# Attention slots of an audio tower: bulk transfers moved out of slots 66 to 100, second-half q and k products moved later

## The reference

```
h = tok(x)                      # rows t, t+3, t+6 side by side (768) times W, plus b: 8 x 744 x 256
h = h + attn(layernorm(h))      # q, k, v products, 16 heads of 16, causal softmax, times Wp, plus bp
h = h + ffn(layernorm(h))       # 4 experts, the best 2 per token by router logits, gelu between w1 and w2
```

## Time and profile before

| | |
|---|---|
| median of 3 runs | 1852.43 us |
| profiled execution | 1851.91 us, its span 1850.2 us |
| TensorE busy | 1545.8 us, 84% |
| VectorE, ScalarE, GpSimd busy | 1098.0, 710.4, 834.7 us |
| granted TensorE clock, mean | 0.904 of full speed |
| DMA | 256.23 MB, mean 138 GB/s |

### The profile page before, as it was taken

How to read it: one execution, slowest core, us unless ns; L and a number is a source line. 1 busy time by engine, 2 the same in 40 slices (tenths; PEclk the granted TensorE clock), 3 DMA queues, 4 the chain that set the end, 5 groups by cost and what they waited for, 6 DMA issues and landing times.

```text
span 1850.2 us, 33109 instructions
## 1 busy us (share of the span) xinstructions
PE 1545.8 (84%) x10648; PEld 1197.0 (65%) x10648; DVE 1098.0 (59%) x3458; ACT 710.4 (38%) x1463; POOL 834.7 (45%) x912
## 2 busy tenths in 40 slices
PE   2679798788798798797797895469999999999997
PEld 2536464464474375464463441469999999999997
DVE  1366668668677577577586680435555555555554
ACT  0114444444444444434444553023333333333332
POOL 4313334634645536536436335324445454544444
PEclk9859899898898898898898886779999999999999
DMA  2241633733724625626526466445554645554551
GB/s 88 77 109 36 166 91 99 191 94 103 195 73 125 166 68 152 142 68 168 126 78 176 109 184 177 126 145 182 179 187 161 205 163 186 167 193 157 191 177 60
DMA packets 166971, 256.23 MB, mean 138 GB/s; under 512 B 30484, under 2 KB 97998, under 8 KB 166800
## 3 DMA queue, kind: packets, MB, share of 16 engines
q1 hardware_dynamic: 108816, 166.66, 31.4%
q10 hardware_dynamic: 34368, 50.33, 9.1%
q0 software_dynamic: 23616, 37.12, 6.7%
HBM read 173.92 MB, written 75.29 MB: 135 GB/s over the span
## 4 chain that ended last, share of the span: by engine, by line
PE 58%; DMA 12%; DVE 10%; issue 9%; POOL 4%; ACT 3%; SPq 3%; ACTq 0%; DVEq 0%; POOLq 0%
PE yb L1384 14%; PE l1b L1371 14%; PE pab L1095 8%; PE pvb L1195 7%; DMA qst<-negp 6%; PE mxb L1155 6%; PE stb L1172 5%; DMA qk_s<-parts 4%; DVE unused L899 3%; SPq L572 2%; PE pab L1137 1%; PE rb L1342 1%; ACT hf L1255 1%; POOL xs L675 1%; POOL parts L703 1%
## 5 line engine op out<-in xcount | busy, mean ns | idle before, releaser
L761 ACT ACTIVATE prob<-stb 124x496 f32<-124x496 f32 (+2 forms) x832 | 402.0, 505 | 453.4 <-PE stb L1172 419.2
L899 DVE CUSTOM_DVE_ANT_0 unused<-mxb,mask_row 124x372 bf16<-124x372 f32 (+4 forms) x768 | 353.7, 484 | 93.3 <-PE mxb L1155 87.4
L1172 PE MATMUL stb<-qst,kst 99*124 99x372 bf16 (+4 forms) x1024 | 319.5, 345 | 97.2 <-DMA qst<-negp 75.1
L1155 PE MATMUL mxb<-kst,qst 96*124 96x372 bf16 (+4 forms) x1024 | 325.2, 349 | 78.1 <-DVE mxp L899 47.5
L1384 PE MATMUL yb<-w2p,hp 128*128 x2448 | 339.2, 284 | 9.9 <-DVE yo L1326 9.9
L1371 PE MATMUL l1b<-x2T,w1s 128*128 128x384 f32 x1632 | 336.4, 341 | 1.2 <-DVE x2T L1285 1.2
L1384 PEld LDWEIGHTS yb<-w2p,hp 128*128 128x128 f32 x2448 | 323.5, 189 | 20.3 <-issue 20.3
L1255 ACT ACTIVATE hf<-l1b,b1c 128x384 f32<-128x384 f32 x272 | 158.3, 582 | 340.0 <-PE l1b L1371 297.1
L1172 PEld LDWEIGHTS stb<-qst,kst 99*124 99x124 bf16 x1024 | 138.0, 145 | 229.1 <-ACT prob L761 85.9
L1371 PEld LDWEIGHTS l1b<-x2T,w1s 128*128 128x128 f32 x1632 | 275.2, 189 | 1.6 <-DVE x2T L1285 1.6
L686 POOL TENSOR_SCALAR_AFFINE_SELECT prob<-prob 124x496 f32<-124x496 f32 x192 | 118.2, 624 | 311.9 <-ACT prob L761 310.9
(11 more groups left out here) (158 smaller groups left out, 1495.1 us busy)
## 6 DMA issues: line engine op xcount, KB each, us to landing
w1s<-ws SPq DMA_DIRECT2D x34, 2048.0 KB, 8.4
qk_s<-parts SPq DMA_DIRECT2D x64, 279.0 KB
xg<-xs SPq DMA_DIRECT2D x34, 396.0 KB
kst<-qk_s SPq DMA_DIRECT2D x32, 279.0 KB, 3.8
qst<-qk_s SPq DMA_DIRECT2D x32, 279.0 KB, 6.5
wraw<-in_w_all ACTq DMA_DIRECT2D x32, 256.0 KB
ws<-whi ACTq DMA_DIRECT2D x32, 256.0 KB
ws<-wlo ACTq DMA_DIRECT2D x32, 256.0 KB
```

The lines of the kernel that those rows point to most:

```text
L761: act.activation(dst, src, ACT.Exp, scale=DH ** -0.5).then_inc(exp_done, 1)
L899: done = dve.tensor_tensor_reduce(out=unused[:, n % 2, e * w:(e + 1) * w], in0=src, in1=mask_row[:, T - w:T], scale=1.0, scalar=-3.0e38, o ...
L1155: done = nc.tensor.matmul(out, qst[g % NG][0:ROWS, h + e, TT * i:TT * i + TT], kst[g % NG][0:ROWS, h + e, k0:k0 + w], start=True, stop=True)
L1172: done = nc.tensor.matmul(out, kst[g][:, h, TT * j:TT * j + TT], qst[g][:, h, q0:q0 + w], start=True, stop=True)
```

## The change

It changes the slots of events and, for `res_load`, the body in which it stands.

| event | slot before | slot after |
|---|---|---|
| `qk` 4 to 7 | 59, 62, 65, 68 | 62, 69, 74, 77 |
| stack of group 2 | 83, for the next batch | 4 of the next body |
| `x_load` | 97 | 35 |
| `res_load` | 73 | 7 of the next body (in the last body 73 as well) |
| `wload` 0 to 3 | 2, 22, 47, 66 | 2, 19, 47, 67 |
| `wsplit` 0 to 3 | 11, 28, 57, 76 | 10, 26, 57, 76 |
| `wstore` 0 to 3 | 17, 34, 63, 85 | 13, 29, 62, 98 |
| `h2_store` | 41 | 42 |

```diff
+        put(4, "late_stack", 2)
         put(19, "late_stack", NG - 1)
...
-        put(41, "h2_store", 0)
+        put(42, "h2_store", 0)
...
-    for n, (load, split, store) in enumerate(((2, 11, 17), (22, 28, 34), (47, 57, 63), (66, 76, 85))):
+    for n, (load, split, store) in enumerate(((2, 10, 13), (19, 26, 29), (47, 57, 62), (67, 76, 98))):
...
-    put(73, "res_load", 0)
+    if not first:
+        put(7, "res_load", -1)
+    if last:
+        put(73, "res_load", 0)
...
-            put(59 + 3 * n, "qk", n + 4)
+            put((62, 69, 74, 77)[n], "qk", n + 4)
         put(51, "load_stack", 0)
         put(72, "load_stack", 1)
-        put(83, "load_stack", 2)
-        put(97, "x_load", 1)
+        put(35, "x_load", 1)
...
                     if kind == "res_load":
-                        if later(b):
-                            act.wait_ge(h2_stored, b * 16)
-                            act.wait_ge(xrow_ready, b * NT)
-                            act.wait_ge(gate_step, b * GATE_STEPS)
-                        act.wait_ge(h1_stored, b * 16 + 16)
-                        act.dma_start(res[:, :, :], h1_s[b].rearrange("(i p) d -> p i d", p=TT)).then_inc(res_loaded, 16)
+                        at = b + n
+                        if later(at):
+                            act.wait_ge(h2_stored, at * 16)
+                            act.wait_ge(xrow_ready, at * NT)
+                            act.wait_ge(gate_step, at * GATE_STEPS)
+                        act.wait_ge(h1_stored, at * 16 + 16)
+                        act.dma_start(res[:, :, :], h1_s[at].rearrange("(i p) d -> p i d", p=TT)).then_inc(res_loaded, 16)
```

## The result

The kernel after takes 1822.57 us, the median of four runs (1820.03 to 1834.66), beside 1854.11 us (1851.38 to 1857.07) for the kernel before: a ratio of 0.9835, with a 95% interval of 0.9809 to 0.9861. The forecast was 1783 us, with a range of 1762 to 1813. The direction was right and the size was not: some 32 us came where 70 were forecast. The profiled execution took 1820.03 us, its span 1818.3 us.

What follows compares the result with a forecast made beforehand. TensorE's score matmuls wait 75.1 us for small DMAs held by bulk transfers, mostly at slots 78 and 0. Terms -41.6 - 12.6 + 0 - 21.7 - 4.2 + 5 + 3 + 2.5 = -69.6 us gave 1783 us, range 1762 to 1813.

Steps and rivals of the forecast that it cites:

- Slot 78: Slot 78, bodies 0 to 6: the wait for the small DMAs goes whole, -41.6 us, and -12.6 us of clock.
- Slot 0: Slot 0, bodies 1 to 7: 0.8 us of wait left where there was more, -21.7 us, and -4.2 us of clock.
- Rival 1: Slot 0: the weight store at 98 holds the small DMAs, 3 us in seven bodies; 1803 us, chance 0.13.
- Rivals 2 and 5: First: slot 78 keeps half its wait, 1810, chance 0.08. Second: transfers aren't what delays the small DMAs, 1852, chance 0.03.
- Slot 52: Slot 52: `h2_store` ahead of its small DMAs comes one slot later, +0.5 us in six bodies, +3 us; bounds 0 and +9.
- The products themselves.: Products moved from slots 59 to 68 into 69 to 77: TensorE and POOL work just fits, 0 us; bounds -3 and +14.
- Rival 3: Slots 69 to 82: POOL binds, masks come late, value products wait 2 to 3 us a body; +17, 1800 us, chance 0.09.
- slots 2 to 35: Slots 2 to 35: group 3's fold copies queue behind the stack, delaying DVE's reciprocal; +0.7 us a body, +5; bounds 0 and +14.
- Tail: Body 7's last w2 loads wait for the later fourth weight store, the last fold behind them: +2.5 us; bounds 0 and +5.
- side estimate: Cold TensorE clock behind DMA waits: the skill's rule, half the throttled time, would make the sum some 5 us lower.

Runs made afterwards that it cites:

- e5: Kernel after with `res_load` back at slot 73 and no longer at 7: 1830.23 us, ratio 0.985 to the kernel before.
- e6: Kernel after with the stack of group 2 back at slot 83 of the body before: 1847.31 us, ratio 0.9932 to the kernel before.
- e13: Kernel after with the h1 store at slot 57 instead of 53 and the third weight store at 70 instead of 62: 1820.37 us, ratio 0.9787.
- e1: Kernel after with products 4 to 7 back at slots 59, 62, 65, 68, all transfers staying moved: 1806.11 us, ratio 0.9721.
- e10: Kernel after with products 4 to 7 back at 59, 62, 65, 68 and the fold of group 0 at slot 49 instead of 45: 1797.73 us, 0.9678.
- e3: Kernel after with the h1 store at slot 80 instead of 53: 1813.43 us, ratio 0.9751 to the kernel before.
- e4: Kernel after with the fourth weight split on POOL at slot 91 instead of 76: 1816.16 us, ratio 0.9767 to the kernel before.
- e9: Kernel after with the fold of group 0 at slot 49 instead of 45, behind product 3's store: 1817.45 us, ratio 0.9763.
- e2: Kernel before with only products 4 to 7 moved, to slots 62, 69, 74, 77: 1851.79 us, ratio 0.9961.
- e8: Kernel after with the stack of group 2 at slot 7 instead of 4, behind the fold of group 3: 1855.08 us, ratio 0.9968.
- e11: Kernel after with the h1 store at slot 57 instead of 53: 1842.14 us, ratio 0.9908 to the kernel before.

## Why the forecast was half right

**What held.** *Slot 78*: forecast for bodies 0 to 6 were -41.6 us of wait and -12.6 of clock. The wait fell from 41.6 to 1.9 us (-39.7), and slots 78 to 84 of these bodies take 10.6 us less, the clock behind the opening at 1.00. The ledger's -47.6 has two things beside that: the 9 us of product 7 that came in, and -3.6 of body 7. *Slot 0*: -25.9 forecast, -35.7 measured: 0.8 us of wait stayed in bodies 1 to 7 where 5.6 were expected, and the clock came back whole. The step at slot 78 was less sure than it looked: in body 3 TensorE was free 5.2 us behind the issue, not 6.7, and the small DMAs needed 5.9, not 5.6, which is the 0.68 us of wait. The mechanism, small DMAs behind bulk on the other queue, stands by e5 and e6. Rival 1 (the weight store holds slot 0) is out, by the five bodies that needed 3.6 us with 512 KB ahead; e13's slot 78 says only that such a store is not harmless where other bulk moves too. Rivals 2 and 5 are out. *Slot 52*: +3 forecast; 6.1 us of wait, less what slots 41 to 51 gained by the same edit (6.9 us). Body 7 did not keep its 5.1 us at slot 78: its `res_load` stands at 73 in all of these kernels, the wait there was 5.14 before, 5.24 in e5 and 1.26 after. TensorE came 2.3 us later, 2.07 of it a wait for a mask at slot 76, and the small DMAs landed 8.4 us after their issue, not 10.0; why, no run shows.

**What failed: "*The products themselves.* ... 0".** The step failed in both of its halves.

The first half followed the products into slots 69 to 77 and asked who is late there. It did not ask who had been covered by the slots they left. Those slots were the cover of group 0's stack, issued behind slot 52 and used at 67, and no wait showed it, since it landed 2 to 3 us early. No term of the sum had this stack at all. The measured price is slot 67's +25.0 us. It is not the products' alone: with them back, 17.2 of 26.5 us of wait stay in e1 and 9.3 us in e10. That part comes from the moved transfers, which alone used up the room, and from the bodies whose product store and h1 store collide (11.7 of e1's 17.2 us, in bodies 1 and 6); with the h1 store away it is gone (e3).

The second half is POOL. Rival 3 had the mechanism and its price, +17; but it had the wrong slots and the wrong chance (0.09). Its sum, 12.5 us of POOL against 12.1 us of TensorE, was 0.4 us over and was taken as fitting, for the sake of the 2 us until the masks of slots 80 and 82. Those are in time; the masks behind the next scatters are not, so slots 84 to 103 pay 18.1 us. The queue behind the sum was not followed that far. There e4, with POOL's split out of the way, gets 15.5 us back, and e1, with the products out of it, 18.7.

Together the step cost some 21 us: e1 against the kernel after (0.9721 against 0.9835, the intervals apart), and 16 by e10 against e9 (0.9678 against 0.9763, the intervals just meeting). By the stretches nearly all of it is POOL's half: slots 90 to 103 make 18.7 of e1's 22 us and 20.1 of e10's 20 us in the profiled executions, and what slot 67 gains with the products back, slots 59 to 67 lose. e2 shows that this is not the products' own cost, for alone they cost nothing; the cost appears once the bulk is gone and with it the waits in which POOL caught up (e5).

**What was sized too small: slots 2 to 35**, +5 with a bound of 14, measured 14.7. The path was named rightly, but over all bodies the reciprocal idled 26.5 us, not 5. In bodies 1 to 6 little of it reached TensorE (4.0 us in slots 11 to 16). Body 7 paid 9.8 us, and the forecast had not looked at it by itself. Its reciprocal and its `proj` at slot 23 in the timeline after:

```profile
1010.54 0.92 DVE L932 RECIPROCAL invs<-sums 48x124 f32<-48x124 f32 x1 [4.76 <-issue]
...
1024.45 2.01 PE L1141 MATMUL pab<-projw,spare 128*124 128x260 f32 x4 [3.78 <-POOL spare L693]
```

*Tail*: +2.5 forecast, +3.6 measured.

**The sum.** Forecast -69.6. With product 7's 9 us counted where they came from: slot 78 -2.4, slot 0 -9.8, slots 11 to 35 +9.7, slots 35 to 59 -9.3, slots 59 to 77 with the stack's wait +26.4, slots 84 to 103 +18.1, the rest (tail, expert stage, start) +4.9: -32. The prediction's side estimate, "some 5 us lower" by the rule it cites, comes to 8 on its own rows (7 x 0.9 at slot 78, half of 4 x 0.8 at slot 0); the sum did not use it. The chances gave faster 0.93, and faster it was; the range ended at 1813 because it held no case of a wait for something other than the small DMAs beyond POOL's.

**What stays open.** Why the small DMAs of slot 0 took 3.8 us in body 3 of the kernel before and 8.2 us in body 2, with the same transfers issued at the same distances ahead. Why in e8 the fold is later with the stack behind it on the queue than ahead of it. Whether the h1 store can be placed between 53 and 80 with neither the stack nor an opening nor a weight store beside it: 57 and 80 were tried, and both pay elsewhere. And the two lengths of the runs of one kernel (e1's four took 1798, 1800, 1813 and 1813 us); in its profiled execution, one of the short ones, three bodies had to wait 8 to 11 us for the product's store, and the number of such bodies in the longer runs was not seen.

## What to carry to other kernels

When a stretch is made shorter, list the loads in flight across it and what each still has in hand when it is used: a load that lands 2 us early makes no wait in the profile, and is the next bound once 3 us are gone. A sum of POOL's work that is as large as TensorE's does not fit because the next consumer is 2 us away; follow the queue to the consumers behind it. And bulk moved out of one window goes into another: price the window where it lands, the issuing engine included, with the same care as the one it leaves.

## What the runs showed of the hardware

- A 279 KB store issued 0.02 us ahead of a 756 KB store on another queue was complete after 9.7 us; issued 1.3 us ahead of it, after 3.0 us (kernel after, bodies 1 and 3). 0.9 us ahead it was complete after 10.4 us in e1's body 1 and after 3.4 us in the kernel after's body 2.
- The issue of a 256 KB DMA can hold its engine: 7.03 and 1.65 us where the pair followed 756 KB by 3.3 us on the same queue, 0.35 and 0.45 us where it followed by 8.1 us (body 3 of e11 and of the kernel after). In bodies 1 to 6 of e11 the first of the two took 6.2 to 7.9 us at 3.2 to 3.6 us behind.
- The six loads of a stack (1116 KB) had landed 7.5 to 8.3 us after the first was issued without the h1 store beside them (e3, bodies 1 to 6), and after 13.3 to 13.8 us with that store of 756 KB 1.7 to 2.8 us ahead on the other queue (kernel after, bodies 2 to 5).
- 512 KB issued about 1 us ahead of three small DMAs did not hold them: they landed after 3.6 us in five of seven bodies, after 4.4 and 4.9 us in the other two (kernel after, slot 0). In body 4 of e13, with more bulk moving, the same 512 KB, 2.9 and 1.2 us ahead, went with 13.3 us.
- Behind a wait of 3.0 us, with the clock at 1.00 before and in it, 0.59 of the clock was granted over the next 4.21 us, all of them busy (slot 67 of body 3, kernel after): part of that stretch was at the lower of the two levels.
